# A three-stage kernel on one Trainium2 core: the first feed-forward's later batches as a list sorted by expert

## The reference

```
x = x + 0.5 * ffn(layernorm(x))
x = x + attention(layernorm(x))      # 16 query heads of 64, one key/value head
x = x + 0.5 * ffn(layernorm(x))      # the same weights

def ffn(x):                          # E = 8 experts, K = 2
    probs = softmax(x @ gate_w + gate_b, axis=1)      # over the 512 tokens of a batch
    vals, idx = top_k(probs, 2)
    h = relu(x @ w1[e] + b1[e]); h = relu(h @ w2[e] + b2[e]); y = relu(h @ w3[e] + b3[e])   # every expert, every token
    w_tok[b, s, e] = vals where e was chosen, else 0
    v[e] = sum over b, s of y[e, b, s] * w_tok[b, s, e]
    out[b, s] = sum of v[e] over the two experts chosen by (b, s)
```

## Time and profile before

| what | us |
|---|---|
| median of 3 runs | 1057.64 |
| the runs | 1049.88, 1057.66, 1057.64 |
| profiled execution, first to last instruction (span) | 1048.3 |
| first reduce to last reduce of the first feed-forward, units 1 to 31 | 39.2 to 176.2 |
| PE busy in the span | 1015.9 |

### The profile page before, as it was taken

How to read it: one execution, slowest core, us unless ns; L and a number is a source line. 1 busy time by engine, 2 the same in 40 slices (tenths; PEclk the granted TensorE clock), 3 DMA queues, 4 the chain that set the end, 5 groups by cost and what they waited for, 6 DMA issues and landing times.

```text
span 1048.3 us, 18768 instructions
## 1 busy us (share of the span) xinstructions
PE 1015.9 (97%) x7176; PEld 661.9 (63%) x7176; DVE 763.9 (73%) x1027; ACT 632.1 (60%) x900; POOL 700.0 (67%) x369
## 2 busy tenths in 40 slices
PE   7999998899999999999999999999999999998996
PEld 6676886545657566556655665745565565776884
DVE  6879998877875676567576587546757636779996
ACT  4785556756754565456475477467746456775553
POOL 5555655766886588488488578756849757565653
PEclk9999999999999999999999999999999999999999
DMA  5721520000100100001001010001000103521612
GB/s 169 237 86 58 183 84 21 1 2 23 42 23 22 42 24 22 22 23 43 22 23 43 3 42 23 22 25 40 22 23 23 42 25 102 182 81 49 209 67 81
DMA packets 30253, 59.62 MB, mean 57 GB/s; under 512 B 10437, under 2 KB 15702, under 8 KB 30166
## 3 DMA queue, kind: packets, MB, share of 16 engines
q1 hardware_dynamic: 30096, 58.41, 18.4%
q10 hardware_dynamic: 70, 0.02, 0.0%
HBM read 55.27 MB, written 2.62 MB: 55 GB/s over the span
## 4 chain that ended last, share of the span: by engine, by line
PE 83%; DVE 10%; ACT 2%; issue 2%; POOL 2%; DMA 0%; DVEq 0%; ACTq 0%; POOLq 0%
PE ring L1038 20%; PE ring L972 6%; PE ring L1050 6%; PE ring L996 5%; PE ring L1002 5%; PE ring L998 5%; PE ring L1000 5%; PE ring L742 4%; PE ring L748 4%; PE ring L744 4%; PE ring L1011 3%; PE ring L766 2%; PE ring L765 2%; PE ring L768 2%; DVE ring L1576 2%
## 5 line engine op out<-in xcount | busy, mean ns | idle before, releaser
L1728 DVE TENSOR_REDUCE mx<-ring 128x2 f32<-128x1024 f32 x248 | 290.3, 1226 | 64.1 <-PE ring L972 64.1
L627 POOL TENSOR_TENSOR sum_picksT<-sum_picksT,P_wb 128x1024 f32<-128x1024 f32 x128 | 310.7, 2427 | 18.9 <-POOL sum_picksT L627 0.9
L1356 ACT ACTIVATE P_wb<-ring 128x1024 f32<-128x1024 f32 x256 | 262.1, 1026 | 54.2 <-PE ring L1002 24.6
L627 POOL TENSOR_TENSOR sum_picksT<-P_wb 128x1024 f32<-128x1024 f32 x64 | 167.0, 2610 | 167.8 <-ACT P_wb L1356 167.8
L686 POOL TENSOR_TENSOR R<-t,R 128x512 fp32r<-128x512 f32 x124 | 162.1, 1308 | 124.5 <-ACT R L1166 121.2
L1038 PE MATMUL ring<-P_wb,t 128*32 128x512 f32 x2048 | 228.4, 593 | 0.0
L1038 PEld LDWEIGHTS ring<-P_wb,t 128*32 128x32 f32 x2048 | 74.0, 110 | 138.6 <-issue 120.0
L1368 ACT COPY OZ<-ring 128x512 f32<-128x512 f32 x64 | 37.4, 585 | 157.3 <-PE ring L1038 148.6
L1166 ACT CAST R<-t 128x512 fp32r<-128x512 f32 x124 | 76.9, 620 | 74.6 <-PE ring L748 68.2
L972 PE MATMUL ring<-R 64*128 64x512 f32 x512 | 104.8, 407 | 1.0 <-ACT P_wb L1344 0.7
L996 PE MATMUL ring<-R 64*128 64x512 f32 x512 | 102.0, 393 | 1.5 <-DVE MR L1733 1.5
(11 more groups left out here) (199 smaller groups left out, 1529.9 us busy)
## 6 DMA issues: line engine op xcount, KB each, us to landing
P_wb<-wd SPq DMA_DIRECT2D x64, 512.0 KB, 4.8
rzb<-rzd SPq DMA_DIRECT2D x64, 256.0 KB, 3.9
xs<-in_L_attn_x SPq DMA_DIRECT2D x8, 256.0 KB, 5.2
zrc<-SZ SPq DMA_DIRECT2D x128, 2.0 KB, 1.7
out<-xs SPq DMA_DIRECT2D x8, 256.0 KB, 2.7
sum_picksT<-in_L_ffn_w SPq DMA_DIRECT2D x2, 512.0 KB, 5.6
MR<-mT SPq DMA_DIRECT2D x62, 4.0 KB
t<-in_L_ffn_w SPq DMA_DIRECT2D x1, 512.0 KB, 7.3
```

What stands on the lines that cost most here:

```text
L627: pool.tensor_tensor(US[:, g % 2, c, :, :], first, PU[:, TPB * c + t, :, :], ALU.add).then_inc(s_ua, 1)
L1356: act.activation(PU[:, u, :, :], ring[slot(("scores", g, u))][:, :, :], ACT.Exp, scale=SCALE).then_inc(s_exp, 1)
L1728: dve.tensor_reduce(mx[:, :, u] if g else mx0_unit[:, u // TPB, :, 0, u % TPB, 0], ring[slot(("max", g, u))][:, :, :], AX.X, ALU.max).then ...
```

## The change

Batches 0 to 3 stay dense (DENSE = 16 units). Batches 4 to 7 are not computed for every expert. Each of their 2048 tokens chose two experts, which makes 4096 rows. The rows are written to a list in DRAM (xg), sorted by expert, each expert's part filled up to whole tiles of TS = 512 rows; RT = 8 + 7 = 15 tiles are enough whatever the choice. Two tiles are a routed unit: RU = 8 units, the last with one tile. So the first feed-forward has 24 units.

New in it, in order of time:

- SP fills xg with zeros, five DMAs from MR, which POOL has cleared. DVE waits for all five before split1 of unit 1.
- ACT writes the normalised rows of batches 4 to 7 to SBUF (rows) beside the row's weights; GATE1 has turns for two batches at once and the four logits in one stage (logits4). The choice is behind units 6 and 7.
- counts and ranks (behind unit 8): PE and DVE work out, for each row, its place in the list, and tile_tables which expert each tile belongs to, with its biases.
- POOL scatters the rows: 32 indirect DMAs of 128 rows, up to six behind each of units 8 to 13. In these units DVE makes the second half of the low part that POOL made before.
- SP waits for all 32, and loads the sorted rows two tiles at a time. gather turns them (8 transposes on PE), ACT makes the high part, DVE the low part and the row weights. SP writes the row weights to DRAM and loads them broadcast.
- POOL copies each tile's expert weights (768 columns a tile) from wex to WT by an index read at run time: four units' ahead of unit 14, then one unit's a step.
- Splits and reduces of routed units are done in halves, since each tile has its own bias.
- The weights are kept in one array wex, by expert, layer and part. The second feed-forward stays dense.

```diff
+    TS = 4 * P
+    DENSE = NU // 2
+    RT = GROUPS * TPB * TPB * P // TS + E - 1
+    RU = (RT + 1) // 2
+    UNITS_OF = (DENSE + RU, NU)
+    ROW = P + E
...
+        def low_by_dve(f, u, k):
+            if f:
+                return k == 1 and u >= NU - 2
+            return u == UNITS_OF[0] - 1 or (k == 1 and SCATTERS.start <= u < SCATTERS.stop)
...
+        SCATTERS = range(8, 14)
         GATE1 = {0: [("moments", 2), ("root", 2)],
-                 1: [("invert", 2), ("normal", 4)],
-                 2: [("turn", 4), ("normal", 5)],
-                 3: [("turn", 5), ("logits", 4), ("normal", 6)],
-                 4: [("turn", 6), ("logits", 5), ("normal", 7)],
-                 5: [("turn", 7), ("logits", 6)],
-                 6: [("logits", 7), ("largest", 1), ("exp", 1)],
-                 7: [("invert_sum", 1), ("probs", 1)],
-                 8: [("turn_probs", 1), ("choose", 0)],
-                 9: [("choose", 1)],
-                 10: [("choose", 2)],
-                 11: [("choose", 3)],
-                 12: [("picks", 1)]}
+                 1: [("invert", 2), ("normal", 4), ("normal", 5)],
+                 2: [("turns", 4), ("normal", 6), ("normal", 7)],
+                 3: [("turns", 6)],
+                 4: [("logits4", 4)],
+                 5: [("invert_sum", 1), ("probs", 1)],
+                 6: [("turn_probs", 1), ("choose", 0), ("choose", 1)],
+                 7: [("choose", 2), ("choose", 3)],
+                 8: [("counts", 1), ("ranks", 1)]}
+        for u in range(SCATTERS.start, SCATTERS.stop):
+            n = u - SCATTERS.start
+            GATE1.setdefault(u, []).extend(("scatter", k) for k in range(6 * n, min(6 * n + 6, 2 * TPB * TPB)))
+        GATE1[SCATTERS.stop - 1] += [("copy", r) for r in range(4)]
+        for r in range(4, RU):
+            GATE1.setdefault(DENSE + r - 4, []).append(("copy", r))
+        GATE1[DENSE].append(("dense_sums", 0))
...
-            for u in range(NU):
-                if u + 2 < NU:
-                    steps += [("layer1", u + 2), ("split", u + 2)]
-                if u + 1 < NU:
-                    steps.append(("layer2", u + 1))
+            last = UNITS_OF[f]
+            for u in range(last):
+                if u + 2 < last and routed(f, u + 2):
+                    steps += [("gather", u + 2), ("layer2", u + 1), ("layer1", u + 2), ("split", u + 2)]
+                else:
+                    if u + 2 < last:
+                        steps += [("layer1", u + 2), ("split", u + 2)]
+                    if u + 1 < last:
+                        steps.append(("layer2", u + 1))
                 steps.append(("layer3", u))
...
+            sp.wait_ge(s_const, 3)
+            for part in range(5):
+                sp.dma_start(xg.rearrange("(p q r) c -> q p (r c)", p=P, q=5)[part], zeros).then_inc(s_zf, 16)
...
+                sp.wait_ge(s_sent, 16 * 2 * TPB * TPB)
+                routed_weights()
...
+            def scatter(n):
...
+                t = n % (TPB * TPB)
+                pool.indirect_dma_start(out=xg[:, :], out_offset=bass.IndirectOffsetOnAxis(ap=row_of[:, n:n + 1], axis=0),
+                                        in_=rows[:, t, :], in_offset=None).then_inc(s_sent, 16)
+
+            def copy_weights(r):
...
+                for k in halves_of(0, DENSE + r):
+                    e = pool.value_load(expert_int[0:1, 2 * r + k:2 * r + k + 1], min_val=0, max_val=E - 1)
+                    ins = pool.tensor_copy(WT[:, r % 4, k, :, :, :].rearrange("p l h o -> p (l h o)"),
+                                           wex[:, bass.ds(e, 1), :, :, :].rearrange("p e l h o -> p (e l h o)"))
...
+            def gather(u):
+                r = u - DENSE
+                k = r % 2
+                pe.wait_ge(s_sorted[k], 16 * (r // 2 + 1))
+                wait_unit(pe, 0, "gather", u)
+                for half in halves_of(0, u):
+                    mm = turn(unit_pair(0, "gather", u)[:, half, :], lambda j: sorted_rows[k][:, half, j, 0:P])
+                mm.then_inc(s_rx, 1)
...
+                dve.wait_ge(s_zf, 16 * 5)
                 split1(0, 1)
...
+            def sorted_low(u):
+                r, n = u - DENSE, len(halves_of(0, u))
+                k = r % 2
+                dve.wait_ge(s_sorted[k], 16 * (r // 2 + 1))
+                wait(dve, s_rwd, 16 * (r - 1))
...
+                choice_link(dve.tensor_tensor(row_products[k][:, 0:n, :, :], sorted_rows[k][:, 0:n, :, P:ROW], tiles, ALU.mult))
+                dve.tensor_reduce(row_weights[k][:, 0:n, :], row_products[k][:, 0:n, :, :], AX.X, ALU.add).then_inc(s_rw, 1)
...
+                dve.wait_ge(s_rxh, r + 1)
+                dve.tensor_tensor(low[:, 0:n, :], unit_pair(0, "gather", u)[:, 0:n, :], high[:, 0:n, :].bitcast(F32), ALU.subtract
+                                  ).then_inc(s_rxl, 1)
```

More of the change, by code:

```diff
@@ L694, in units @@
                         x_low(f, arg)
+                    elif stage == "scatter":
+                        scatter(arg)
+                    elif stage == "copy":
+                        copy_weights(arg)
             def add_update(f, b):
@@ L889, in units @@
                         layer3(f, arg)
+                    elif stage == "gather":
+                        gather(arg)
                     elif stage in UNIT_USES:
@@ L894, in units @@
                             sums(arg, bank)
+                        elif stage == "turns":
+                            turn_rows(arg, bank)
+                            turn_rows(arg + 1, other)
+                        elif stage == "logits4":
+                            for b in range(TPB, B):
+                                logits(f, b, bank)
+                        elif stage == "counts":
+                            pe.wait_ge(s["wtk_ready"], 2)
+                            turn_indicators(bank[:, 0:2 * P]).then_inc(s["picks_transposed"], 1)
+                            pe.matmul(other[:, 0:NT * E], ones[:, :], wtk[:, :, :, :].rearrange("p g e t -> p (g e t)"),
+                                      start=True, stop=True).then_inc(s["picks_transposed"], 1)
+                            pe.wait_ge(s["wtk_ready"], 3)
+                            pe.wait_ge(s_const, 5)
+                            pe.matmul(other[:, NT * E:NT * E + E], ones[:, :], chosen_by_p, start=True, stop=True)
+                            pe.matmul(other[:, NT * E + E:NT * E + 2 * E], before, chosen_by_p, start=True, stop=True).then_inc(s["picks_transposed"], 1)
+                        elif stage == "ranks":
+                            pe.wait_ge(s_ind_taken, f + 1)
+                            pe.wait_ge(s_mask, 1)
+                            pe.matmul(bank[:, 0:P], indT[:, 1, :], before_same, start=True, stop=True).then_inc(s["picks_transposed"], 1)
                         elif stage == "turn":
@@ L1256, in attention_normal, with normal_rows, sorted_high @@
                 normal(b, s_axn, 0)
+            def normal_rows(b):
+                for j in range(TPB):
+                    t = TPB * b + j
+                    ins = act.activation(rows[:, t - TPB * TPB, 0:P], xs[:, t, :], ACT.Identity, bias=nmr[:, t:t + 1], scale=rstd[:, t:t + 1])
+                ins.then_inc(F[0]["xn_done"], 1)
+            def sorted_high(u):
+                r = u - DENSE
+                n = len(halves_of(0, u))
+                act.wait_ge(s_rx, r + 1)
+                wait(act, F[0]["l1_done"], u - 1 if r >= 2 else 0)
+                act.copy(x_of(0, u)[0][:, 0:n, :], unit_pair(0, "gather", u)[:, 0:n, :]).then_inc(s_rxh, 1)
             def normal(b, done, home=None):
@@ L1454, in _ @@
                 dve.memset(prio[:, e:e + 1], float(E - e))
+            for i in range(2 * E):
+                dve.memset(count_up[:, i:i + 1], float(i))
+            for buffer in running:
+                dve.memset(buffer[:, 0:TPB], 0.0)
             ln_count = [0]
@@ new lines, in place_rows @@
+            def place_rows(ranks):
+                (_, _, oh1, oh2), t = GW[0][1]["small"], TPB * TPB
+                dve.wait_ge(F[0]["picks_transposed"], 5)
+                dve.tensor_tensor(row_of_all, ranks.rearrange("p (t e) -> p t e", e=E), first_row.unsqueeze(1).to_broadcast([P, t, E]), ALU.add
+                                  ).then_inc(s_places, 1)
+                dve.wait_ge(s_places, 2)
+                for k, chosen in enumerate((oh1, oh2)):
+                    ins = dve.tensor_tensor(by_batch(products[:, k, :, :]), by_column(chosen), by_batch(row_of_all), ALU.mult)
+                choice_link(ins)
+                choice_link(dve.tensor_reduce(row_sums, products, AX.X, ALU.add))
+                dve.tensor_copy(row_of, row_sums.rearrange("p k t -> p (k t)")).then_inc(s_places, 1)
@@ L1653, in units @@
                     elif stage == "layer3":
[L1654 to L1655 removed]
+                        split2(f, arg)
                         reduce3(f, arg)
+                    elif stage == "gather":
+                        sorted_low(arg)
```

(11 more changed lines are left out.)

436 lines of the change are left out of this document (317 added, 119 removed).

## The result

| | before | after |
|---|---|---|
| median, us | 1054.91 (4 runs, 1049.88 to 1057.66) | 1099.58 (4 runs, 1097.98 to 1102.1) |
| ratio | | 1.0438, 95% interval 1.0396 to 1.048 |
| span of the profiled execution | 1048.3 | 1096.1 |
| sum over units / tiles, start | 176.33 | 220.29 |

The change makes the kernel 44.7 us slower, by the medians. The forecast was +23.9 us, 1081.5: the direction was right and the measured 1099.6 lies in the wide range (1058 to 1110), but not in the narrow one that I gave for my own case (1066 to 1097), and the size was about half of what came. The two profiled executions differ by 47.8 us, of which 43.96 lie ahead of the sum over tiles; the loss is nearly all in the stretch that the prediction worked through.

What follows compares the result with a forecast made beforehand. PE, busy 1015.9 of 1048.3 us, was taken as the bound. First gather at 135.4 plus 64.8 us put the sum over tiles at 200.2 against 176.33: +23.9 us, 1081.5, with 8 in 10 for 1058 to 1110.

Steps and rivals of the forecast that it cites:

- my own case: The prediction's main case for the whole kernel: 1081.5 us, range 1066 to 1097 with scatters of 0.8 to 1.5 us; chance 0.62.
- split of unit 1, by the zero fill: Early on DVE: the split waits for the zeros to land in DRAM, +2 us, 0 to 5 possible.
- unit 8's reduce: On DVE after gate and choice: starts at 82.3 us, from 76.75 plus 2 for the fill and 3.5 net.
- POOL from the first scatter to the last: During units 9 to 13: 32 scatters of 1.1 us and five low halves of 1.29, 41.7 us, done at 129.5.
- first gather: On PE after SP's wait and load: starts at 135.4 us, 5.9 us after POOL is done.
- start-up step: First routed step: turn, cast, low half, layer 1, split and reduce in a row, 11.1 us.
- six routed steps: Routed units after the start-up: DVE's chain, waiting for layer 1, takes 7.4 us a step, 44.4 us in all.
- half step, tail, sum: End of the routed part: half step 4.4, last two reduces with last layers 4.5, sum over tiles 0.4 us more.
- behind the sum: Update, attention and second feed-forward after the sum over tiles: nothing changes, 0 us.
- Cheap scatters: Rival for POOL's scatters: 0.46 us each, DVE's pace rules units 9 to 13, +9.7 us, 1067; chance 0.20.
- Dear scatters: Rival for POOL's scatters: 2.36 us each, or held up on POOL's side, +64 us, 1122; chance 0.12.
- The faster rival: Routed steps at PE's 5.3 us, gather, cast and low half a step ahead, with cheap scatters: -17.7 us, 1040; chance 0.06.

Runs made afterwards that it cites:

- removal runs: Against the changed kernel, left out 16 of the 32 scatters (1080.49 us) or all 32 with SP's wait for them (1073.17 us).
- sized transposes: Changed kernel plus dummy transposes on PE, 130 ahead of the first gather and 14 ahead of each routed layer 1: 1091.53 us.
- reduces later: Changed kernel with each reduce of units 14 to 21 put on DVE between the low half of the unit three later and its split: 1090.22 us.
- weights in a row: Changed kernel with the routed reduce reading its token weights from SBUF in one piece, the step of four on the PSUM side: 1088.58 us.
- half the scatters: Changed kernel with every second scatter left out (16 of 32), those rows staying zero, and SP waiting for 16: 1080.49 us.
- the run without scatters and with POOL's low halves: Changed kernel without the 32 scatters, both low halves of units 8 to 13 on POOL again: 1065.77 us.
- the form without scatters: Changed kernel without scatters, POOL's low halves back, reduce, weight, dense-layer, low-part and copy-wait edits together, 10 transposes a step: 1061.94 us.

## Why the prediction was right, and where it was short

| step of the prediction | forecast | measured |
|---|---|---|
| split of unit 1, by the zero fill | +2 | +0.36 (27.08 to 27.44) |
| unit 8's reduce | 82.3 | 81.11 |
| row numbers ready | 87.8 | 86.2 |
| POOL from the first scatter to the last | 41.7 | 47.9 (86.53 to 134.47) |
| first gather | 135.4 | 139.56 |
| start-up step | 11.1 | 10.0 |
| six routed steps | 44.4 | 56.6 (149.56 to 206.11) |
| half step, tail, sum | 9.3 | 14.2 (to 220.29) |
| behind the sum | 0 | +3.8 |

The misses add up: the first gather 4.2 us later than forecast, the start-up 1.1 shorter, the six steps 12.2 longer, the tail 4.9 and what lies behind the sum 3.8 longer, in all 23.9, the 47.8 us between the two spans less the 23.9 that were forecast. The mechanism was right, but that 1099.6 is within 1058 to 1110 is in part luck: the upper end was made for scatters of 2 us, and half of the excess came from the steps, a good part of the rest from the tail and what lies behind it.

**Zero fill, gate and choice: right.** The five DMAs were issued from 11.3 us on, not 15 to 16, and landed in time but for 0.40 us. The head terms together, up to the row numbers, were 1.6 us too dear.

**Scatters: mechanism right, term too small.** "I take ... 1.1 us": it is 1.26, 32x0.16 = 5.1 us, and POOL had six low halves between them, not five, 1.3 more. The sum 32x1.26+6x1.27 = 47.9 is what the trace shows. My guess (a little less than POOL's 128x512) was within 12% of the busy time but left out the 0.30 us to the next one. The 1 us of the Trainium skill, page "DMA: Bandwidth & Descriptors", section "Latency and other measured facts", is near the busy 0.98; it is there a time to the first byte and not one of POOL's, so the agreement may be chance, and the gap isn't in it. The removal runs bear out that the scatters are on the path: 16 fewer brought vv 17.0 us forward, all 32 26.2 (counted from unit 8's reduce); the rest of their 40.3 us is covered, since DVE's pace of 5.2 us holds these units anyway.

**"Sum 7.4 us" for a routed step: this is the term that was furthest off.** The order of events was right, the sizes were not. Worked out from DVE's rows for the six steps (12.2 us over):

- The waits for layer 1 came to 14.0 us instead of 6x1.65 = 9.9, so 4.1. Of this 3.5 go with the low granted clock, which I had charged to the start-up alone (shown by the sized transposes, where the waits are 10.5).
- The row products with the row weights took 0.87 on the mean instead of 0.35, so 3.1. The single product is 0.21 undisturbed and 0.65 to 0.92 in the five steps in which it ends 0.1 us behind an instruction of POOL; that POOL is the cause was tried by an edit only for the low half in the tail.
- The routed reduces took 5x0.63 more, less 0.3 in the first step, which still has a dense one: 2.9 (shown by the order of the weights).
- The sums of the dense part, once 1.6, were forgotten though the diff lists them. Two of their three instructions, 0.90 and 0.52 us for 128x8, also end with one of POOL's.
- The splits took 0.7 more, the low halves 0.4 less.

Together 12.0.

**Tail: 4.9 us too cheap.** Five strided reduces 1.9, the collision with POOL's query weights 1.7; 1.3 stays unexplained. **"Nothing changes" behind the sum:** nothing did in the work, but the update ran at half PE's clock after the tail's gaps (0.50 from 220 to 232; before it was 1.00 from 176 to 188), and 3.8 us came. What lies behind the sum in the span is 872.0 us before and 875.8 after. In the other traces with the same tail it goes with the granted clock of the first 12 us behind the sum: 872.2 us at 0.77 (reduces later), 873.4 at 0.72 (weights in a row), 873.7 to 874.2 at 0.58 to 0.60 (four runs), 875.9 at 0.50 (half the scatters); the run without scatters and with POOL's low halves, 874.9 at 0.75, doesn't fit. That the clock alone makes the difference was not tried.

**The clock.** The granted clock was 0.50 from 134 to 140, inside PE's idle stretch of 16.7 us, and on through the first gather. It also fell among the routed steps, where PE's longest holes were 1.8 to 2.7 us, once a step: 0.87 on the mean from 140 to 206. That is what the forecast left out; its +1.5 us for the start-up was too dear, since with the clock at 1.00 (sized transposes) the start-up took 9.45 us instead of 10.0. For the fall after an idle stretch the prediction cited the Trainium skill, page "TensorE: Matmul & The Clock Gate", section "What's actually happening"; the trace agrees (0.50).

**Rivals.** Cheap scatters fell by the 0.96 us of the rows. Dear scatters (2.36) fell the same way. The faster rival, steps at PE's pace of 5.3 us, fell in the form without scatters: a step took 7.30, and even without its two waits and without the 0.5 us that the row product loses beside POOL, DVE has 5.9 us of work in it. Its condition itself, the cast a whole step ahead, was never built: DVE still waited 0.54 us for ACT. The medians of the kernel before also moved between runs by some us (1050.6 to 1054.9 against the 1057.64 shown at first), which enters the difference of 44.7.

## What to carry to other kernels

Before work is taken off the busiest engine, count what each unit of the new form costs every other engine: here 35.6 us of PE work went, but a step that DVE paces at 7.3 us left less than 9 us to win, against 26 us for the scatters alone. A chain through four engines doesn't run at anybody's pace, and here its gaps also lowered PE's clock, so a step's forecast wants the wait at both clocks. And price each new instruction by its operands: the order in SBUF changed DVE's time by half, and what POOL read beside it made short instructions 3 to 18 times as long.

## What the runs showed of the hardware

- An indirect DMA of 128 rows of 544 bytes costs POOL 0.96 us and 0.30 more to the next one, with 32 of them as with 16. DVE's low halves with two SBUF inputs stayed at 0.68 us beside them.
- A DVE instruction with two SBUF inputs waits for a POOL instruction that reads SBUF and began first: 0.69 became 2.38, 0.29 became 2.01, 0.21 became 3.78 beside eight copies. Where DVE's began 0.22 us ahead of POOL's (weights in a row), it stayed at 0.69, and POOL's took 2.68 instead of 2.35. The Trainium skill, page "SBUF — State Buffer", section "SBUF: two separate sides", says that VectorE and GpSimd share a pair of SBUF ports as an exclusive lock, that a VectorE instruction with two SBUF inputs needs it against a GpSimd one that reads SBUF, and that "the other fully blocks". The rows agree: in the three long cases the DVE instruction ended 0.1 to 0.5 us behind POOL's.
- DVE reading one fp32 SBUF operand at a step of four values (16 bytes) took 1.14 us for 128x512 instead of 0.75; the same step on the PSUM operand and output cost nothing. The Trainium skill, page "SBUF — State Buffer", section "Door 1: The DMA port swizzle", gives SBUF lines of 16 bytes and a penalty for each new one; the rows agree, and put the price at half of the instruction.
- 200 fp32 transposes of 128x128 took 23.4 us, 0.117 each. Put into PE's holes, 130 ahead of the first gather and 14 a step, they held the granted clock at 1.00 from 140 to 206 us, a stretch that had 0.87 without them.
